# Two graph attention layers on one core: the first layer's product in three f16 parts from packed words in one ring of eight slots

## The chip, the cores and the metric

One Trainium2 chip, one of its cores. The metric is device time in microseconds (us) of one execution, the median of the runs. TensorE is PE in the rows (PEld is its weight load), VectorE is DVE, ScalarE is ACT, GpSimd is POOL, and SyncE is SP, whose queue issues the loads of the adjacency matrix.

## What is computed

x is 8192 x 128 in f32, adj is 8192 x 8192 of 0 and 1 in int32. Cut to what matters:

```python
def layer0(h, adj, W, a):
    wh = h @ W
    e = wh @ a[:128] + (wh @ a[128:]).T
    e = jnp.where(e > 0, e, 0.2 * e)
    att = softmax(jnp.where(adj > 0, e, -9e15), axis=-1)
    return elu(att @ wh)

def layer1(f, adj, Wq, Wk):
    Qn, Kn = unit_rows(f @ Wq.T), unit_rows(f @ Wk.T)
    att = softmax(jnp.where(adj > 0, Kn @ Qn.T, -9e15), axis=1)
    prop = where(row_has_edge, att @ f, f)
    return 0.5 * prop + 0.5 * f

x = x + layer0(relu(layernorm(x)), adj, W, a)
x = x + layer1(relu(layernorm(x)), adj, Wq, Wk)
```

With e = a_i + b_j, the exponential of the leaky sum is the greater of exp(a_i + b_j) and exp(0.2 a_i + 0.2 b_j). Up to a factor of row i, which the quotient of the softmax removes, that is exp(b_j) times the greater of r_i = exp(0.8 a_i) and a threshold of column j, exp(-0.8 b_j). So layer 0 needs no exponential for each pair (i, j).

## The kernel before

**Stages.** LayerNorm of x, a transpose and the projection with W (to about 46 us of the profile), layer 0 (52 to 992 us), the second LayerNorm's transposes and the q and k projections (to about 1075 us), and layer 1 (to the end, 2463.6 us). The change touches layer 0 and the head of it.

**Layer 0.** The 8192 rows i are cut in 8 chunks of 1024 (`C0`), each with 8 accumulators of 128 x 129 in PSUM (`acc0`; two sets, so that the next chunk can start while one is read). For each chunk the kernel goes over the 8192 neighbours j in 64 tiles of 128, two tiles to a step; so a chunk has 32 steps, and layer 0 has 256. A step loads 1 MB of adj into `adj_ring` (4 slots), makes 2 x 1024 weights per partition in `p_ring` (4 slots, f32), and multiplies them with two tiles of `v_buf` (wh with a column of ones, f32).

**Who does what in a step.** DVE makes the weights of the even tile (L762, two per-partition scalars) and then multiplies both tiles by the mask adj > 0 (L770, 2048 elements in one instruction, which counts `s_p` up). ACT makes the odd tile in two operations (L452, L456). PE waits for `s_p` and issues 16 f32 products (L982), 8 row blocks for each tile; each shows in the records as two matmuls and two weight loads. It then counts `s_used` up. After a chunk PE adds a term for rows without an edge (L998, 8 f32 products) and counts `s_acc` up.

**The epilogue of a chunk** (quotient, elu, residual, LayerNorm, split into two f16 halves for layer 1) is cut into pieces that DVE and ACT do between the steps of the next chunk: on DVE `denominators` (L692), `negative` (L697), `residual` (L701, L704), `moments` (L710), `scales` (L609) and `split` (L723, L725), on ACT `quotient` (L403), `exponential` (L409), `root` (L415, with a table load) and `normalised` (L425). In chunk 0 their places on DVE hold eight column sums of `v_buf` (L742).

**SP's queue.** A slot of `adj_ring` is free as soon as DVE has masked it, so a load (L250) waits for `s_p`. At the start of a chunk SP first issues the chunk's first four loads, and then the row factors of the next chunk (L266, 512 KB, a row broadcast to 128 partitions), for which it waits until DVE is through with the chunk before. ACT turns them into r_i (L389). For chunk 0 the row factors don't pass through memory: PE transposes them to PSUM (L949).

**Layer 1** already multiplies in f16 halves: scores (L1050, 512 columns), and then, for each row block, high x high, high x low, low x high (L1067, 129 or 128 columns, weights next to each other in memory). In both layers the loop over chunks is unrolled by two, with a shorter loop inside.

## Time and profile before

| | |
|---|---|
| median of 3 runs | 2465.29 us (2465.23 to 2467.15) |
| span of the profiled execution | 2463.6 us |
| PE busy | 2390.4 us, 97% |
| weight loads busy | 2006.0 us, 81% |
| DVE busy | 2133.0 us, 87% |
| ACT busy | 1756.8 us, 71% |
| DMA in layer 0 | about 300 GB/s, 85% of 16 engines busy |

The span is from the first to the last instruction; the runs' time lies 1.7 us above it. Busy shares are averages over stages; the rows ahead of the prediction are read by stage.

### The profile page before, as it was taken

How to read it: one execution, taken by the hardware profiler on the slowest of the kernel's cores; microseconds unless marked ns; L12 is line 12 of the kernel's file. 1: busy time of each engine (PE TensorE's matmuls, PEld its weight loads, DVE VectorE, ACT ScalarE, POOL GpSimd, SP SyncE). 2: the span in 40 equal slices, each digit the busy share in tenths (PEclk: the TensorE clock that was granted, in tenths of full speed). 3: DMA queues.
4: the chain of work that ended last, by engine and by line, in shares of the span. 5: the costliest groups of instructions: out<-in, count | busy, mean ns of one | idle time of the engine just before them, and what ended most of it. 6: DMA issues, size and time to landing. Idle time of an engine off the chain costs nothing.

```text
span 2463.6 us, 62421 instructions
## 1 busy us (share of the span) xinstructions
PE 2390.4 (97%) x24203; PEld 2006.0 (81%) x24203; DVE 2133.0 (87%) x1653; ACT 1756.8 (71%) x1654; POOL 1.4 (0%) x9
## 2 busy tenths in 40 slices
PE   6999999999999999799999999999999999999999
PEld 5899999999999999667776776776767767767777
DVE  7989898989898988898887888888888878878887
ACT  6567676777777776677776776776777767767776
POOL 0000000000000000000000000000000000000000
PEclk9999999999999999999999999999999999999999
DMA  4798888888888879245565665655655556556563
GB/s 184 256 323 295 304 293 309 304 303 307 299 309 287 318 281 327 68 151 204 203 216 180 210 213 178 217 205 190 213 201 201 202 188 217 192 197 215 205 205 120
DMA packets 153299, 572.05 MB, mean 232 GB/s; under 512 B 9872, under 2 KB 10320, under 8 KB 152784
## 3 DMA queue, kind: packets, MB, share of 16 engines
q1 hardware_dynamic: 143952, 549.26, 63.7%
q10 hardware_dynamic: 9216, 20.98, 2.2%
q8 instruction: 91, 1.49, 0.2%
q14 instruction: 40, 0.33, 0.0%
HBM read 557.58 MB, written 12.62 MB: 231 GB/s over the span
## 4 chain that ended last, share of the span: by engine, by line
PE 91%; DVE 4%; issue 3%; ACT 1%; DMA 0%; SPq 0%; DVEq 0%; ACTq 0%
PE bank L982 35%; PE bank L1067 28%; PE bank L1050 27%; DVE v_sum L742 1%; PE bank L998 1%; DVE hl_buf L620 1%; DVE p_ring L762 0%; DVE hl_buf L802 0%; DVE p_ring L632 0%; PE bank L1009 0%; DVE norm L791 0%; DVE v_buf L809 0%; DVE q_buf L809 0%; PE bank L928 0%; DMA wqk_sb<-wqk 0%
## 5 line engine op out<-in xcount | busy, mean ns | idle before, releaser
L982 PE MATMUL bank<-v_buf,p_ring 128*128 (+1 forms) x8192 | 920.2, 275 | 10.5 <-DVE p_ring L770 6.0
L982 PEld LDWEIGHTS bank<-v_buf,p_ring 128*128 128x128 f32 x8192 | 917.8, 192 | 12.2 <-issue 10.9
L529 ACT ACTIVATE p_ring<-bank 128x1024 f32<-128x1024 f32 x512 | 523.8, 1024 | 386.2 <-PE bank L1050 386.0
L1067 PEld LDWEIGHTS bank<-u_buf,hl_buf 128*128 128x128 f16 x12288 | 721.7, 97 | 61.9 <-issue 2.2
L835 DVE SCALAR_TENSOR_TENSOR p_ring<-adj_ring,p_ring 128x2048 f32<-128x2048 int32 x256 | 586.6, 2292 | 204.4 <-ACT p_ring L529 204.4
L1067 PE MATMUL bank<-u_buf,hl_buf 128*128 (+2 forms) x12288 | 742.7, 220 | 1.2 <-issue 1.1
L1050 PE MATMUL bank<-v_buf,q_buf 128*128 (+1 forms) x3072 | 711.1, 381 | 21.2 <-issue 19.1
L770 DVE SCALAR_TENSOR_TENSOR p_ring<-adj_ring,p_ring 128x2048 f32<-128x2048 int32 x255 | 584.6, 2292 | 75.6 <-DVE p_ring L762 29.9
L840 DVE TENSOR_TENSOR hl_buf<-p_ring,hl_buf 128x2048 f16<-128x2048 f32 x256 | 584.6, 2284 | 0.0
L1050 PEld LDWEIGHTS bank<-v_buf,q_buf 128*128 (+1 forms) x3072 | 291.8, 98 | 329.1 <-issue 29.6
L535 ACT ACTIVATE hl_buf<-p_ring 128x2048 f16<-128x2048 f32 x256 | 487.1, 1903 | 0.6 <-DVE p_ring L835 0.6
L452 ACT ACTIVATE p_ring<-r_ring,ns_col,f_col 128x1024 f32<-128x1024 f32 x256 | 317.6, 1241 | 222.3 <-PE bank L982 211.6
L456 ACT ACTIVATE p_ring<-p_ring,s_col 128x1024 f32<-128x1024 f32 x256 | 294.3, 1150 | 29.6 <-ACT p_ring L452 12.2
L762 DVE TENSOR_SCALAR p_ring<-r_ring,f_col,s_col 128x1024 f32<-128x1024 f32 x256 | 206.7, 808 | 9.5 <-PE bank L982 4.1
L1009 PE MATMUL bank<-wqk_sb,hl_buf 128*128 128x256 f32 x128 | 33.7, 410 | 10.0 <-DVE hl_buf L802 8.9
L1009 PEld LDWEIGHTS bank<-wqk_sb,hl_buf 128*128 128x128 f32 x128 | 24.3, 200 | 16.5 <-ACT hl_buf L471 7.2
L914 PE MATMUL bank<-ident,hl_buf 128*128 128x128 f32 x128 | 20.9, 292 | 9.9 <-DVE hl_buf L620 9.8
L914 PEld LDWEIGHTS bank<-ident,hl_buf 128*128 128x128 f32 x128 | 15.7, 148 | 13.7 <-DVE hl_buf L620 8.3
L403 ACT ACTIVATE hl_buf<-bank,den 128x128 f32<-128x128 f32 x64 | 17.2, 377 | 12.1 <-DVE den L692 12.1
L425 ACT ACTIVATE hl_buf<-q_buf,nbias,rstd 128x128 f32 (+1 forms) x64 | 25.8, 483 | 0.0
L1020 PE MATMUL bank<-ident,hl_buf 128*128 128x128 f32 x128 | 17.7, 283 | 5.7 <-DVE v_buf L809 5.7
L544 ACT ACTIVATE r_ring<-bank,den 128x128 f32<-128x128 f32 x64 | 18.1, 371 | 6.7 <-DVE den L857 6.7
(94 smaller groups left out, 432.6 us busy)
## 6 DMA issues: line engine op xcount, KB each, us to landing
adj_ring<-adj SPq DMA_DIRECT2D x512, 1024.0 KB, 4.9
x_dram<-q_buf ACTq DMA_DIRECT2D x8, 512.0 KB, 5.5
h_dram<-hl_buf ACTq DMA_DIRECT2D x8, 512.0 KB, 5.7
hl_buf<-h_dram SPq DMA_DIRECT2D x16, 256.0 KB, 2.7
r_ring<-x_dram ACTq DMA_DIRECT2D x16, 256.0 KB, 3.7
r_ring<-h_dram ACTq DMA_DIRECT2D x16, 256.0 KB, 3.9
out<-r_ring ACTq DMA_DIRECT2D x16, 256.0 KB, 3.8
r_ring<-a_rows SPq DMA_DIRECT2D x7, 512.0 KB, 5.5
```

The lines of the kernel that those rows point to most:

```text
L452: nc.scalar.activation(dst, row, ACT.Relu, bias=ns_col[:, bass.ds(j, 1)], scale=f_col[:, bass.ds(j, 1)]).then_inc(s_half, 1)
L456: nc.scalar.activation(dst, dst, ACT.Identity, bias=s_col[:, bass.ds(j, 1)]).then_inc(s_odd, 1)
L529: nc.scalar.activation(p_ring[:, k, hf * 1024:(hf + 1) * 1024], bank[:, 2 * hf:2 * hf + 2, :].rearrange("p b n -> p (b n)"), ACT.Exp, scal ...
L535: nc.scalar.activation(hl_buf[:, 0, k, :], p_ring[:, k, :], ACT.Copy).then_inc(s_ph, 1)
L762: V.tensor_scalar(p0(k)[:, :, 0, :], row, f_col[:, bass.ds(j, 1)], s_col[:, bass.ds(j, 1)], ALU.mult, ALU.max).then_inc(s_even, 1)
L770: V.scalar_tensor_tensor(p_ring[:, k, :], adj_ring[:, k, :], 0.0, p_ring[:, k, :], ALU.is_gt, ALU.mult).then_inc(s_p, 1)
L835: V.scalar_tensor_tensor(p_ring[:, k, :], adj_ring[:, k, :], 0.0, p_ring[:, k, :], ALU.is_gt, ALU.mult).then_inc(s_m, 1)
L840: V.tensor_tensor(hl_buf[:, 1, k, :], p_ring[:, k, :], hl_buf[:, 0, k, :], ALU.subtract).then_inc(s_pl, 1)
L982: ins = mm(acc0(par, it), p0(k)[:, it // 4, jj, f], v_buf[:, bass.ds(j * VW, D + 1)], start=start, stop=False, skip_group_check=True)
L1009: ins = mm(qk_banks(r)[:, k * 2 * D:(k + 1) * 2 * D], ht_ring[:, r, k * P:(k + 1) * P], wqk_sb[:, :], start=True, stop=True)
L1050: ins = mm(bank[:, 2 * hf + m, :], q_buf[:, qs, bass.ds(j * P, P)], k_buf[:, ks, bass.ds(i * IW, IW)], start=(x == 0), stop=(x == 2))
L1067: ins = mm(o, hl_buf[:, ps, k, f], v.rearrange("p o c -> p (o c)"), start=head and m == 0 and it % 2 == 0 and (ps, us) == (0, 0), stop=tai ...
```

## The change

**Weights.** The r_i and the thresholds become words of 32 bits: the upper 16 bits are an f16 just below the value (value times 1 - 2^-11), the lower 16 bits are the f16 of what is left (`split_words`). Of two such positive words the greater as an f32 is the word of the greater value. In a step ACT turns the slot's 0 and 1 into 0.0 and 1.0 in place (`ACT.Sign`, 2048 elements), and DVE takes, for each of the two tiles, max(row word, threshold word) * mask in place (two SCALAR_TENSOR_TENSOR of 1024 elements with one per-partition scalar). So a slot holds adj, then the mask, then the weights: there is one `ring` of 8 slots in the place of `adj_ring` and `p_ring`, and layer 1 uses its two halves as before.

**Values.** exp(b_j) goes into the values: `value_scaled`, `value_high` and `value_low` (DVE, ACT, DVE; 16 times each, 4 tiles at a time) turn each tile of `v_buf` into two f16 halves. Two of the 16 are done before the first step, the others between the steps of chunk 0.

**Products.** For each tile PE does 8 row blocks high x high, then 8 high x low, then 8 low x high, all f16 with 129 columns. The weights are read from the words, so each f16 weight lies 4 bytes from the next. The column sums (L742) go: ACT sums the columns of h as it copies them (`accum_out`), DVE adds those sums up, and PE multiplies them with W.

**Queues.** A slot is free when PE has used it, so a load waits for `s_used`. The load of the next chunk's row words is written ahead of the chunk's first loads. The row words of chunk 0 go through memory too. PE's groups in the loop are 8 steps long (they were 4), and the chunks' steps on ACT and DVE are written out without an inner loop.

```diff
-                    for k in range(RING):
-
-                        sp.wait_ge(s_p, RING * (G0 * c + g - 1) + k + 1)
-                        load0(c, RING * g + k, k)
+                    for k in range(RING0):
+
+                        sp.wait_ge(s_used, U0 * c + RING0 * (g - 1) + k + 1)
+                        load0(c, RING0 * g + k, k)
+
+                if not last:
+                    if not first:
+
+                        sp.wait_ge(s_p, U0 * c)
+                    load_r(c + 1, 1 - par)
                 if not first:
                     group(0)
-                if not last:
-                    if not first:
-
-                        sp.wait_ge(s_p, RING * G0 * c)
-                    load_r(c + 1, 1 - par)
...
+                for u in range(U0):
+                    k = u % RING0
+                    act.wait_ge(s_adj[k], 16 * (G0 * c + u // RING0 + 1))
+                    act.nop(nofuse=True)
+                    nc.scalar.activation(slot(k), slot(k, I32), ACT.Sign).then_inc(s_sg, 1)
+                    if u in parts:
+                        parts[u]()
...
+                dve.wait_ge(s_rin[par], 8 * c + 16 - 8 * par)
+                dve.nop(nofuse=True)
+                for u in range(U0):
+                    k = u % RING0
+                    n = U0 * c + u
+                    dve.wait_ge(s_sg, n + 1)
+                    dve.nop(nofuse=True)
+                    for jj in range(2):
+                        half = words0(k)[:, :, jj, :]
+                        ins = V.scalar_tensor_tensor(half, r_ring[:, par, :].rearrange("p (b n) -> p b n", b=2),
+                                                     th_word[:, 2 * u + jj:2 * u + jj + 1], half, ALU.max, ALU.mult)
+                    ins.then_inc(s_p, 1)
+                    if u in parts:
+                        parts[u]()
...
+            def value_scaled(q):
+                if q >= 2:
+                    dve.wait_ge(s_vl, q - 1)
+                f4 = f_col[:, ZT * q:ZT * q + ZT].unsqueeze(2).to_broadcast([P, ZT, D + 1])
+                V.tensor_tensor(vz_ring[:, q % 2, :, :], v0[:, ZT * q:ZT * q + ZT, 0:D + 1], f4,
+                                ALU.mult).then_inc(s_vz, 1)
+
+            def value_low(q):
+                dve.wait_ge(s_vh, q + 1)
+                tiles = v2_tiles[:, ZT * q:ZT * q + ZT, :]
+                V.tensor_tensor(tiles[:, :, VW:VW + D + 1], vz_ring[:, q % 2, :, :], tiles[:, :, 0:D + 1],
+                                ALU.subtract).then_inc(s_vl, 1)
...
+                            for ps, us in parts:
+                                for it in range(IT0):
+                                    start = peeled and k == 0 and jj == 0 and it % 3 == 0
+                                    f = slice((it % 4) * P, (it % 4 + 1) * P)
+                                    ins = mm(acc0(par, it), weights0(k, ps)[:, it // 4, jj, f],
+                                             v2[:, bass.ds((2 * j + us) * VW, D + 1)],
+                                             start=start and (ps, us) == (0, 0), stop=False, skip_group_check=True)
```

The order of the work moves on two queues that the prediction speaks of. On SP, at the start of the loop over pairs of chunks, this stands there before (`weights_ready` is `s_p`, which DVE counts; L250 loads adj, L266 the row factors):

```order
L216 ISA
L278 REGISTER_ALU
L250 ISA [waits weights_ready]
L250 DMA adj_ring<-adj 128x2x1024
L278 REGISTER_ALU
L250 ISA [waits weights_ready]
L250 DMA adj_ring<-adj 128x2x1024
...
L286 REGISTER_ALU
L266 ISA [waits weights_ready]
L266 DMA r_ring<-a_rows 128x1024
```

And this now (`weights_used` is `s_used`, which PE counts; L266 loads adj, L282 the row words):

```order
L232 ISA
L282 ISA [waits weights_ready]
L282 DMA r_ring<-a_rows 128x1024
L296 REGISTER_ALU
L266 ISA [waits weights_used]
L266 DMA ring<-adj 128x2x1024
L296 REGISTER_ALU
L266 ISA [waits weights_used]
L266 DMA ring<-adj 128x2x1024
```

The wait for DVE and the load of the row words moved from behind the chunk's first loads to ahead of them.

On DVE, at the start of chunk 0's steps, this stands there before (L762 and L770 as above, L742 a column sum):

```order
L762 TENSOR_SCALAR p_ring<-r_ring,f_col,s_col 128x2x512
L770 SCALAR_TENSOR_TENSOR p_ring<-adj_ring,p_ring 128x2048 [waits adj_in1,odd_tile_ready,even_tile_ready]
L742 TENSOR_REDUCE v_sum<-v_buf 128x16
L762 TENSOR_SCALAR p_ring<-r_ring,f_col,s_col 128x2x512
L770 SCALAR_TENSOR_TENSOR p_ring<-adj_ring,p_ring 128x2048 [waits adj_in2,odd_tile_ready,even_tile_ready]
```

And this now (L781 the max and mask of one tile, L707 `value_scaled`, L713 `value_low`):

```order
L707 TENSOR_TENSOR hl_buf<-v_buf,f_col 128x516 [waits factors_ready,words_step]
L707 TENSOR_TENSOR hl_buf<-v_buf,f_col 128x516
L713 TENSOR_TENSOR v_buf<-hl_buf,v_buf 128x4x129 [waits values_high] x2
L781 SCALAR_TENSOR_TENSOR ring<-r_ring,th_word,ring 128x2x512 [waits r_in0,mask_ready]
L781 SCALAR_TENSOR_TENSOR ring<-r_ring,th_word,ring 128x2x512
L707 TENSOR_TENSOR hl_buf<-v_buf,f_col 128x516 [waits values_low]
L781 SCALAR_TENSOR_TENSOR ring<-r_ring,th_word,ring 128x2x512 [waits mask_ready]
L781 SCALAR_TENSOR_TENSOR ring<-r_ring,th_word,ring 128x2x512
L713 TENSOR_TENSOR v_buf<-hl_buf,v_buf 128x4x129 [waits values_high]
```

A step has two equal instructions now, and one piece of the values stands behind each step of the first 28.

On PE, the loop body over pairs of chunks holds 2320 f16 products (400 f32 products before), and the shorter loop inside it 384 (64 before).

## Rows read from the trace of the kernel before

**Rows 1.** PE in order of time, layer 0: start us, duration us, engine, line, operation

```profile
118.96 57.44 PE L982 MATMUL bank<-v_buf,p_ring 128*128 x512 [0.80 <-DVE p_ring L770]
176.24 1.95 PE L998 MATMUL bank<-v_sum,empty_w 128*128 128x129 f32 x16
178.02 114.52 PE L982 MATMUL bank<-v_buf,p_ring 128*128 128x129 f32 x1024
292.38 1.95 PE L998 MATMUL bank<-v_sum,empty_w 128*128 128x129 f32 x16
294.17 114.52 PE L982 MATMUL bank<-v_buf,p_ring 128*128 128x129 f32 x1024
...
991.92 1.89 PE L1009 MATMUL bank<-wqk_sb,hl_buf 128*128 128x256 f32 x8
```

**Rows 2.** PE in order of time, two stretches of layer 1

```profile
1202.11 2.75 PE L1050 MATMUL bank<-v_buf,q_buf 128*128 x12
1204.70 2.90 PE L1067 MATMUL bank<-u_buf,hl_buf 128*128 x48
1207.44 2.75 PE L1050 MATMUL bank<-v_buf,q_buf 128*128 x12
...
1317.38 4.39 PE L1050 MATMUL bank<-v_buf,q_buf 128*128 x12 [3.24 <-issue]
1321.56 3.00 PE L1067 MATMUL bank<-u_buf,hl_buf 128*128 128x129 f16 x48
```

**Rows 3.** DVE in order of time, the epilogue's pieces in chunk 3 of layer 0

```profile
429.99 0.69 DVE L697 TENSOR_SCALAR hl_buf<-hl_buf 128x1024 f32<-128x1024 f32 x1
430.59 0.81 DVE L762 TENSOR_SCALAR p_ring<-r_ring,f_col,s_col 128x1024 f32<-128x1024 f32 x1
...
440.38 1.22 DVE L701 SCALAR_TENSOR_TENSOR hl_buf<-hl_buf 128x1024 f32<-128x1024 f32 x1
441.75 1.23 DVE L704 SCALAR_TENSOR_TENSOR q_buf<-hl_buf,q_buf 128x1024 f32 x1 [0.16 <-DVE hl_buf L701]
442.89 0.81 DVE L762 TENSOR_SCALAR p_ring<-r_ring,f_col,s_col 128x1024 f32<-128x1024 f32 x1
```

**Rows 4.** Groups by line: engine, operation, shapes, count | busy us, mean ns | idle before, releaser

```profile
L770 DVE SCALAR_TENSOR_TENSOR p_ring<-adj_ring,p_ring 128x2048 f32<-128x2048 int32 x255 | 584.6, 2292 | 75.6 <-DVE p_ring L762 29.9 <-ACT p_ring L456 18.4 <-issue 18.0
L535 ACT ACTIVATE hl_buf<-p_ring 128x2048 f16<-128x2048 f32 x256 | 487.1, 1903 | 0.6 <-DVE p_ring L835 0.6
L1050 PE MATMUL bank<-v_buf,q_buf 128*128 (+1 forms) x3072 | 711.1, 381 | 21.2 <-issue 19.1 <-ACT p_ring L529 1.2 <-DVE hl_buf L802 0.9
L867 DVE SCALAR_TENSOR_TENSOR r_ring<-r_ring,den 128x128 f32<-128x128 f32 x64 | 18.1, 346 | 0.0
L874 DVE TENSOR_TENSOR r_ring<-r_ring 128x512 f32<-128x512 f32 x16 | 11.0, 685 | 0.0
```

**Rows 5.** All engines in order of time, the head of layer 0

```profile
45.74 0.27 DVE L665 TENSOR_REDUCE ab_max<-v_buf 128x1 f32<-128x64 f32 x1 [5.43 <-ACT v_buf L354]
47.61 0.27 ACT L378 ACTIVATE hl_buf<-bank 64x128 f32<-64x128 f32 x1 [1.90 <-PE bank L952]
47.90 0.55 SPq L260 DMA_DIRECT2D a_rows<-hl_buf  x1
49.77 0.35 SPq L266 DMA_DIRECT2D r_ring<-a_rows  x1
52.04 9.01 PE L982 MATMUL bank<-v_buf,p_ring 128*128 128x129 f32 x64 [4.47 <-DVE p_ring L737]
```

**Rows 6.** DMA issues from 46 to 56 us: KB each, median us from issue to landing

```profile
r_ring<-a_rows SPq DMA_DIRECT2D x1, 512.0 KB, 3.6
```

**Rows 7.** DMA issues from 1090 to 2440 us

```profile
adj_ring<-adj SPq DMA_DIRECT2D x247, 1024.0 KB, 4.8
```

**Rows 8.** Busy time in stretches: length, engines (x instructions), PEclk, DMA share, GB/s

```profile
178.02:294.17 116.15, 116.15 (x1042) 116.15 (x1041) 104.37 (x89) 85.89 (x86) 0.00 (x0) 1.00 0.83 300
412.00:416.00 4.00, 4.00 (x38) 4.00 (x37) 3.84 (x6) 1.75 (x2) 0.00 (x0) 1.00 0.97 349
956.00:960.00 4.00, 4.00 (x38) 4.00 (x37) 3.96 (x4) 2.82 (x3) 0.00 (x0) 1.00 1.04 411
1318.00:1322.00 4.00, 4.00 (x16) 1.70 (x15) 0.00 (x0) 1.22 (x2) 0.00 (x0) 0.57 0.32 130
```

More of the change, by code:

```diff
@@ L32 @@
 RING = 4
+RING0 = 8
 LAG = 3
@@ L347, in copy_h1t @@
                     act.wait_ge(s_wh, g - 1)
-                nc.scalar.activation(ht_ring[:, g % 2, :], bank[:, g % 2, :], ACT.Relu).then_inc(s_h1c, 1)
+                nc.scalar.activation(ht_ring[:, g % 2, :], bank[:, g % 2, :], ACT.Relu,
+                                     accum_out=h_sums[:, g:g + 1]).then_inc(s_h1c, 1)
             def evac1(g):
@@ L436, in chunk @@
                 first = isinstance(c, int) and c == 0
-                last = isinstance(c, int) and c == NC0 - 1
-                parts = {} if first else {(g + 1, 1): part for g, part in enumerate(epilogue(c - 1, 1 - par))}
-                if not last:
-                    parts[SPREAD - 1, 1] = lambda: row_factor(c + 1, 1 - par)
-                def group(g, peeled=False):
-                    for k in range(RING):
-                        n = RING * (G0 * c + g) + k
-                        j = 2 * (RING * g + k) + 1
-                        if not (first and peeled):
-                            act.wait_ge(s_used, n - RING + 1)
-                            act.nop(nofuse=True)
-                        dst = p0(k)[:, :, 1, :]
-                        row = r_ring[:, par, :].rearrange("p (b n) -> p b n", b=2)
-                        nc.scalar.activation(dst, row, ACT.Relu, bias=ns_col[:, bass.ds(j, 1)],
-                                             scale=f_col[:, bass.ds(j, 1)]).then_inc(s_half, 1)
-                        act.wait_ge(s_half, n + 1)
-                        act.nop(nofuse=True)
-                        nc.scalar.activation(dst, dst, ACT.Identity, bias=s_col[:, bass.ds(j, 1)]).then_inc(s_odd, 1)
-                        if isinstance(g, int) and (g, k) in parts:
-                            parts[g, k]()
                 if first:
-                    act.wait_ge(s_r, 1)
-                else:
-                    act.wait_ge(s_r, c + 1)
-                for g in range(SPREAD):
-                    group(g, peeled=(g == 0))
-                with act.Fori(0, G0 - SPREAD) as h:
-                    group(h + SPREAD)
+                    parts = {2 * q - 3: (lambda q=q: value_high(q)) for q in range(2, T // ZT)}
+                    value_high(0)
+                    value_high(1)
+                else:
+                    parts = dict(zip((5, 9, 13, 17), epilogue(c - 1, 1 - par)))
+                for u in range(U0):
[5 more added lines that the diff above has]
+                        parts[u]()
             def copy_ht(g, r):
@@ L678, in _ @@
-            V.tensor_scalar(shift[:, 1:2], shift[:, 0:1], 1.0 - ALPHA, 0.0, ALU.mult, ALU.max).then_inc(s_ab, 1)
-            dve.wait_ge(s_ab, 10)
-            V.tensor_tensor(shift[:, 3:4], shift[:, 3:4], shift[:, 1:2], ALU.subtract).then_inc(s_ab, 1)
-            V.tensor_tensor(shift[:, 4:5], shift[:, 4:5], shift[:, 1:2], ALU.subtract).then_inc(s_ab, 1)
+            top_a, top_nb, top_b = (ab_top[:, i:i + 1] for i in range(3))
+            V.tensor_scalar(ab_col[:, 0, :], ab_col[:, 0, :], top_nb, None, ALU.min).then_inc(s_ab, 1)
@@ new lines, in chunk @@
+                if first:
+                    parts = {2 * q - 4: (lambda q=q: value_scaled(q)) for q in range(2, T // ZT)}
+                    parts |= {2 * q - 3: (lambda q=q: value_low(q)) for q in range(2, T // ZT)}
+                    value_scaled(0)
+                    value_scaled(1)
+                    value_low(0)
+                    value_low(1)
+                else:
+                    parts = dict(zip((3, 7, 10, 11, 15, 19), epilogue(c - 1, 1 - par)))
+                dve.wait_ge(s_rin[par], 8 * c + 16 - 8 * par)
```

219 lines of the change are left out of this document (98 added, 121 removed).

## The prediction

> **What bounds the kernel now.** I read the order of time on PE first. In layer 0 PE works without a gap: a chunk is 114.4 us of L982 and 1.8 us of L998, together 116.15 us, from one chunk's first product to the next's (178.02 to 294.17) [rows 1]. That is 1024 records at 111.7 ns, so 223.4 ns for an f32 product and 3.57 us for a step of 16. In the same stretch DVE is busy 104.4 us, ACT 85.9 us, and the DMA engines move 300 GB/s at a share of 0.83 [rows 8]. So layer 0 goes at PE's pace, with DVE 10% behind it. The stages after it start at 991.92 us [rows 1]; the change leaves them alone, so all that counts is by how much that mark moves.
>
> **PE: the products.** The nearest row for three f16 parts is L1067 in layer 1: 48 products from 1204.70, and the next scores start at 1207.44 [rows 2]. That is 2.74 us, 57.1 ns for a product with its weight load. A step of the changed layer 0 is also 48 f16 products, so 2.74 us, and a chunk is 32 x 2.74 + 1.78 = 89.5 us instead of 116.15. What no row shows is a weight load whose f16 elements lie 4 bytes apart. From below it costs nothing more. From above I take the pace of f32 weight loads, which also read 4 bytes for an element: 111.7 ns. I take 57.1, since both the type and the number of weights are those of L1067.
>
> The Trainium skill, "TensorE: Matmul & The Clock Gate", section "Back-to-back issue gap", puts a sustained stream of pairs of weight load and matmul at about 81 ns each for 128 columns. By it a step would be 3.89 us, above the 3.57 us of f32, and the change would lose 80 us. L1067's row, the same stream but for the spacing of the weights, says 57.1 ns, so the row decides.
>
> **DVE: two instructions a step.** Before, a step is L762 and L770. Now it is two SCALAR_TENSOR_TENSOR of 1024 elements. L704 is one of that size: it starts at 441.75 and the next instruction at 442.89, a pitch of 1.14 us [rows 3]. The new one has a per-partition scalar as well. L867 has one too, at 128 elements: 18.1 us busy for 64, a pitch of 283 ns [rows 4]. Scaled by (1024 - 128) elements at 0.96 a ns that is 1.22 us. So a step is 2.28 to 2.44 us; I take 2.43, as L867 is the same form. The epilogue of a chunk adds its pieces as they show now: 0.6 us for L697, 2.5 us for L701 with L704 [rows 3], and in the same way 0.2, 2.6, 0.3 and 2.0 us for the others, 8.2 us. DVE needs 32 x 2.43 + 8.2 = 86.0 us for a chunk, 3.5 us under PE. ACT's one operation has 2048 elements, as L535: 1.90 us [rows 4], so 61 us and the epilogue's 10. If integer input made it as slow as two of L452 (2 x 1.24 us) it would still be under PE. Pieces that ACT and DVE hand to each other I put at 1.5 us a chunk in waits for DVE (0 to 3).
>
> **SP: what the moved load costs.** This is the step on which the forecast turns. Call D the moment at which DVE ends the last step of a chunk. In the new order SP stands at the wait for D before it may issue the row words, and the next chunk's first loads stand behind them. Their slots came free long before: DVE runs ahead of PE by a few us at most, so at D PE has ended all but two or three of the chunk's steps, and the slots of four or five are free. None of their loads is on its way. From D the chain is: the row words land 3.6 us after their issue when the queue is empty [rows 6]; the load behind them adds 1 MB at the full rate, 2.54 us at 411 GB/s [rows 8]; so it lands at D + 6.3. (From its own 4.8 us [rows 7], the issue of the row words and their 1.3 us of data it comes to 6.8, near enough.) ACT's mask takes 1.95 us with its signal and DVE 2.5 us: the first step of the new chunk is ready at D + 10.9, where it would have been D + 2.4. The next three come at the pace of the loads, 2.54 us. Then DVE goes on at its own pace. From D to the next D:
>
> 10.9 + 3 x 2.54 + 28 x 2.43 + 8.2 + 1.5 = 96.2 us.
>
> That is above PE's 89.5 us, so DVE's chain with the late loads sets the pace of chunks 1 to 6. Chunk 7 has no row words to wait for and goes at PE's pace. PE hides a part of D's delay only where it lags behind DVE; here it catches up in the epilogue, where DVE needs 47.1 us for 16 steps and pieces and PE 43.8 us, and gets 11 x 0.31 = 3.4 us behind again by the chunk's end.
>
> **Head and chunk 0.** Before, PE starts at 52.04 [rows 5]. Now: the row factors on ACT (L378 at 47.61) come some 0.8 us later, behind more small DVE operations; two more of these split them, 0.5 us; the write takes 1.87 us from issue to the next issue (47.90 to 49.77) [rows 5], the row words 3.6 us [rows 6]. DVE starts its first step at 54.4, and PE at 57.0: 5 us later than before. In chunk 0 DVE also has 28 pieces of the values, 516 elements each, 0.62 us by L874 (685 ns [rows 4], less the 0.07 us that neighbours overlap): D at 54.4 + 32 x 2.43 + 17.4 = 149.6. These 17.4 us lie on the path, since nothing covers them.
>
> **Instruction fetch.** The loop over pairs of chunks in layer 1 has PE wait for "issue" 3.24 us once each 175 us, when it goes back, and the next scores take 4.39 us instead of 2.75 [rows 2] at a granted clock of 0.57 [rows 8], a mean of its two levels (1.2 and 2.4 GHz) after the idle time: 4.8 us in all. Layer 0's loop body grows beyond that of layer 1, so it will pay the same, twice, at a chunk's end. There PE waits for the late loads anyway, some 3 us, and it has slack in the epilogue, so I put it at nothing; without that cover it is 9.6 us. The inner loop (384 products) would be fetched anew only if the memory for it were smaller than I think: layer 1's inner loop of 240 also goes back, twice in each of 16 chunks, and all of L1050's waits for issue are 19.1 us [rows 4], six gaps like the one shown.
>
> The Trainium skill, "Runtime: NRT & Kernel Launch", section "Instruction fetch mechanics", gives PE 2048 instructions, which fits both observations, but also speaks of two pages of 16 KiB, by which the inner loop would be fetched anew, 8 times.
>
> **The sum.** D of chunk 0 at 149.6; six periods of 96.2 us give 726.8. PE is 3.4 us behind there, ends its step and L998 (4.5 us), and does chunk 7 in 87.7 + 1.8 + 1.0 us (with the two transposes): 825.2 us. Before it is 991.9. So 166.7 us less: a span of 2296.9 us, and with the 1.7 us that the median lies above the span, **2299 us**. With DVE's step at 2.34 and the delay 1 us shorter it is 2275, with 2.50 and 3 us of waits 2320; that is the likeliest case's own range.
>
> **Rivals.**
> *PE's pace holds.* If DVE's steps take 2.28 us, or the loads come sooner, every chunk is 89.5 us. Chunk 0 ends on PE at 154.2; 154.2 + 7 x 89.5 + 9.6 + 1.0 = 791 us, and the kernel takes 2265 us. For it: PE's row is firm, and DVE is under PE but for the delay. Against it: 8.5 us of delay in each of six chunks against 3.5 us of slack.
> *DVE or the DMA queue is dearer.* At 2.55 us a step it is 28 x 0.12 x 6 + 4 = 24 us more, 2323. The DMA queue must move 32 MB of adj, 1 MB of results and 0.5 MB of row words in a chunk. At 411 GB/s that is 85.5 us; at the 349 GB/s of another full stretch (share 0.97) [rows 8] it is 100.7 us, 4.5 us above the period, 27 us in all, 2326. Both together give 2350. For it: of the two stretches with the queue full that I show, one is that slow. Against it: the other, as long, moves 411.
> *The inner loop is fetched anew.* 8 x 4.8 = 38 us on PE, of which the slack of six chunks takes most: up to 2320, within the cases above.
> *Slower than before: the spaced weights.* If a weight load with 4 bytes between elements is paced like an f32 one, a step is 48 x 111.7 = 5.36 us and the change loses 256 x (5.36 - 3.57) = 458 us: 2923. It decides from 74.5 ns a product on. For it: no row has such a load. Against it: nothing in the rows but the likeness to L1067.
> *The change doesn't do what it says.* If the products went in as f32 pairs or the mask held the slots up, time would stay near 2465; I see nothing for it.
>
> **How the numbers follow.** The forecast (2275 to 2320) has 0.50, PE's pace (2250 to 2275) 0.19, the dearer case (2320 to 2350) 0.24, the spaced weights 0.05, and no effect or a mishap 0.02. The range from 2256 to 2342 leaves out the spaced weights, no effect, and the outermost parts of the two neighbours. A measurement of this kernel can tell 0.2% from no change. Faster by more than that: 0.94; within it 0.01; slower 0.05.
>
> **What would show it.** Right: PE's L982 successor at 57 ns a product; in chunks 1 to 6 a wait of DVE for ACT's mask of some 8 us after the 32nd step, with ACT waiting for DMA, and SP's longest waits on DVE; a period of about 96 us, but 90 in chunk 7. Wrong: a period of 90 us everywhere (PE's pace), a DMA share of 1.0 through the whole chunk (the queue), products well above 57 ns apart (spacing), or waits of "issue" in the middle of a chunk (fetch).

## The result and the profile after

The changed kernel takes 2316.4 us (three executions, 2316.0 to 2318.0) against 2466.2 us (2465.2 to 2467.3): a ratio of 0.9393, interval 0.9378 to 0.9408, 6.1% faster. A fourth execution, of 7992.7 us, is left out as disturbed; with it the median is 2317.2. The forecast was 2299 us with a range of 2256 to 2342. So sign and range held, and the kernel is 17 us slower than forecast. The profiled execution has a span of 2314.2 us; 2296.9 was worked out.

The page of the changed kernel: busy time of the engines, the chain that ended last, and the groups that answer to [rows 4]:

```profile
PE 2195.6 (95%) x28293; PEld 1803.8 (78%) x28293; DVE 1981.7 (86%) x1685; ACT 1632.2 (71%) x1423; POOL 1.4 (0%) x9
...
PE 70%; DVE 13%; issue 8%; DMA 5%; ACT 3%; SPq 0%; DVEq 0%; ACTq 0%; POOL 0%; POOLq 0%
...
L985 PE MATMUL bank<-v_buf,ring 128*128 128x129 f16 (+1 forms) x12288 | 719.6, 222 | 57.7 <-DVE ring L781 55.9
...
L1052 PE MATMUL bank<-v_buf,q_buf 128*128 (+1 forms) x3072 | 713.2, 382 | 21.5 <-issue 19.2
L781 DVE SCALAR_TENSOR_TENSOR ring<-r_ring,th_word,ring 128x1024 f32<-128x1024 f32 x512 | 622.0, 1279 | 89.4 <-ACT ring L464 85.3
...
L464 ACT ACTIVATE ring<-ring 128x2048 f32<-128x2048 int32 x256 | 481.1, 1911 | 131.4 <-DMA ring<-adj 127.2
```

The products of layer 0 are L985 now. They are busy 719.6 us, where the f32 products before filled eight chunks of 114.5 us [rows 1]. But PE stands idle 55.9 us ahead of them for DVE (L781), DVE stands idle 85.3 us for ACT's mask (L464), and ACT 127.2 us for the loads of adj. The row of L1052, in layer 1, is what it was in [rows 4] but for 2 us.

PE in order of time, layer 0, for [rows 1]; in brackets the idle time just before and what ended it. A row names a stretch of one line, xcount is how many matmuls are in it:

```profile
57.42 95.00 PE L985 MATMUL bank<-v_buf,ring 128*128 128x129 f16 x1536 [9.60 <-DVE ring L781]
152.26 2.00 PE L1002 MATMUL bank<-v_sum,empty_w 128*128 128x129 f32 x16
161.99 34.60 PE L985 MATMUL bank<-v_buf,ring 128*128 128x129 f16 x576 [7.73 <-DVE ring L781]
197.59 21.96 PE L985 MATMUL bank<-v_buf,ring 128*128 x384 [1.00 <-DVE ring L781]
...
351.98 2.00 PE L1002 MATMUL bank<-v_sum,empty_w 128*128 128x129 f32 x16
359.71 34.72 PE L985 MATMUL bank<-v_buf,ring 128*128 128x129 f16 x576 [5.73 <-DVE ring L781]
...
748.57 2.00 PE L1002 MATMUL bank<-v_sum,empty_w 128*128 128x129 f32 x16
750.41 65.54 PE L985 MATMUL bank<-v_buf,ring 128*128 128x129 f16 x1152
...
840.31 1.89 PE L1013 MATMUL bank<-wqk_sb,hl_buf 128*128 128x256 f32 x8
```

From the end of chunk 0 (154.10, 1.84 us after L1002 begins, as between 748.57 and 750.41) to the first product of chunk 7 (750.41) it is 596.3 us, 99.4 for each of the chunks 1 to 6. Each of them begins with a gap of 4.4 to 7.7 us, ended by DVE. Chunk 7 (750.41 to 840.31) has no gap and takes 89.9 us, where a chunk took 116.15 before. The next stage starts at 840.31, not at 991.92 [rows 1]; 825.2 was worked out.

SP's waits (us in total, times, longest):

```profile
SPq L266 <- PE bank L985: 478.7, 199, 11.2
SPq L282 <- DVE ring L781: 90.1, 6, 18.5
```

L282 is the load of the row words. Six times, 15.0 us each on average, SP stands there until DVE has ended the last step of a chunk, with the next chunk's first loads behind it. All engines in order of time show what that costs, at the start of chunk 2:

```profile
243.86 2.48 DVE L781 SCALAR_TENSOR_TENSOR ring<-r_ring,th_word,ring 128x1024 f32<-128x1024 f32 x2
...
246.51 0.34 SPq L282 DMA_DIRECT2D r_ring<-a_rows  x1
247.12 9.80 SPq L266 DMA_DIRECT2D ring<-adj  x8
...
254.76 1.91 ACT L464 ACTIVATE ring<-ring 128x2048 f32<-128x2048 int32 x1 [14.31 <-DMA ring<-adj]
256.77 6.41 DVE L781 SCALAR_TENSOR_TENSOR ring<-r_ring,th_word,ring 128x1024 f32<-128x1024 f32 x5 [10.44 <-ACT ring L464]
...
259.31 3.00 PE L985 MATMUL bank<-v_buf,ring 128*128 128x129 f16 x26 [4.42 <-DVE ring L781]
```

DVE ends chunk 1 at 246.34 (the forecast's D). SP issues the row words 0.2 us later and then loads of adj, seven of them within 5 us; the profile shows a wait for PE only ahead of the eighth. So most slots had been free before their loads were issued. The first has landed at 254.76, when ACT starts, having waited 14.3 us. This is D + 8.4; the forecast had D + 6.3. DVE starts at 256.77 and has the first step, two instructions at a pitch of 1.196 us, at 259.2: D + 12.8 instead of D + 10.9.

In chunks 1, 3 and 5 one more thing lies in this chain. The same view, chunk 3, where D is 345.43:

```profile
353.87 1.28 ACT L464 ACT_TABLE_LOAD   x1 [14.09 <-DMA ring<-adj]
```

Behind an ACT_TABLE_LOAD of 1.28 us the first step is ready at D + 14.1. Over the six chunks it is 13.5, 12.8, 14.1, 13.0, 14.3 and 13.1 us, on average 13.5.

Windows for [rows 8] (length, then busy time of PE, PEld, DVE, ACT, POOL with instructions, PE's granted clock, DMA share, GB/s):

```profile
154.10:252.89 98.79, 89.43 (x1539) 88.93 (x1537) 84.66 (x88) 69.13 (x52) 0.00 (x0) 0.97 0.91 359
360.00:364.00 4.00, 4.00 (x43) 4.00 (x41) 4.00 (x4) 2.81 (x2) 0.00 (x0) 0.54 1.02 406
649.23:748.57 99.34, 91.90 (x1555) 91.23 (x1553) 91.64 (x94) 77.94 (x57) 0.00 (x0) 0.97 1.02 405
748.57:838.47 89.90, 89.90 (x1564) 89.88 (x1561) 78.53 (x83) 62.94 (x52) 0.00 (x0) 1.00 0.96 372
```

DMA issues from 180 to 740 us, for [rows 6, 7] (KB each, median us to landing):

```profile
ring<-adj SPq DMA_DIRECT2D x183, 1024.0 KB, 9.3
...
r_ring<-a_rows SPq DMA_DIRECT2D x5, 512.0 KB, 4.4
```

In chunk 1 no engine is busy for the whole 98.8 us: PE is busy 89.4, DVE 84.7, ACT 69.1. After its gap PE also runs slowly, at a granted clock of 0.54 in 360 to 364, a mean near the lower of its two levels (1.2 and 2.4 GHz). A load of adj lands 9.3 us after its issue, where one in layer 1 took 4.8 [rows 7]. The DMA queue is full outside SP's standstill: its share is 0.91 over chunk 1 and 1.02 over chunk 6 (649.23 to 748.57), at whose end there is no standstill. Both chunks are nearly equally long, so the queue doesn't set the period.

### The profile page after: what moved, and what is told of

The parts are those of the page before. It is cut to its first block, busy times and chain, and to the rows that moved or that the text cites. A ratio compares the mean times of both kernels' runs of the same rounds, so it can differ in the third digit from the quotient of the medians.

```text
span 2314.2 us, 69259 instructions
## 1 busy us (share of the span) xinstructions
PE 2195.6 (95%) x28293; PEld 1803.8 (78%) x28293; DVE 1981.7 (86%) x1685; ACT 1632.2 (71%) x1423; POOL 1.4 (0%) x9
## 3 DMA queue, kind: packets, MB, share of 16 engines
q8 instruction: 155, 2.54, 0.4%
## 4 chain that ended last, share of the span: by engine, by line
PE 70%; DVE 13%; issue 8%; DMA 5%; ACT 3%; SPq 0%; DVEq 0%; ACTq 0%; POOL 0%; POOLq 0%
PE bank L1069 30%; PE bank L1052 29%; PE bank L985 10%; DVE ring L781 9%; DMA ring<-adj 4%; ACT ring L464 1%; ACT hl_buf L440 1%; DVE hl_buf L806 1%; DVE stats L742 0%; DVE norm L795 0%; SPq L266 0%; ACT hl_buf L418 0%; DVE hl_buf L733 0%; PE bank L1013 0%; DVE v_buf L813 0%
## 5 line engine op out<-in xcount | busy, mean ns | idle before, releaser
L528 ACT ACTIVATE ring<-bank 128x1024 f32<-128x1024 f32 x512 | 523.8, 1024 | 387.5 <-PE bank L1052 387.3
L985 PE MATMUL bank<-v_buf,ring 128*128 128x129 f16 (+1 forms) x12288 | 719.6, 222 | 57.7 <-DVE ring L781 55.9
L985 PEld LDWEIGHTS bank<-v_buf,ring 128*128 128x128 f16 x12288 | 713.0, 99 | 64.5 <-DVE ring L781 34.2
L839 DVE SCALAR_TENSOR_TENSOR ring<-ring 128x2048 f32<-128x2048 int32 x256 | 586.6, 2291 | 205.8 <-ACT ring L528 205.8
L1052 PE MATMUL bank<-v_buf,q_buf 128*128 (+1 forms) x3072 | 713.2, 382 | 21.5 <-issue 19.2
L781 DVE SCALAR_TENSOR_TENSOR ring<-r_ring,th_word,ring 128x1024 f32<-128x1024 f32 x512 | 622.0, 1279 | 89.4 <-ACT ring L464 85.3
L844 DVE TENSOR_TENSOR hl_buf<-ring,hl_buf 128x2048 f16<-128x2048 f32 x256 | 584.5, 2283 | 0.0
L464 ACT ACTIVATE ring<-ring 128x2048 f32<-128x2048 int32 x256 | 481.1, 1911 | 131.4 <-DMA ring<-adj 127.2
L1052 PEld LDWEIGHTS bank<-v_buf,q_buf 128*128 (+1 forms) x3072 | 292.0, 98 | 330.9 <-issue 32.2
L534 ACT ACTIVATE hl_buf<-ring 128x2048 f16<-128x2048 f32 x256 | 487.1, 1903 | 0.6 <-DVE ring L839 0.6
L440 ACT ACTIVATE hl_buf<-q_buf,nbias,rstd 128x128 f32 (+1 forms) x64 | 25.9, 485 | 14.3 <-DVE nbias L610 14.3
L408 ACT ACTIVATE v_buf<-hl_buf 128x516 f16<-128x516 f32 x16 | 10.2, 641 | 27.1 <-DVE hl_buf L707 27.1
L918 PEld LDWEIGHTS bank<-ident,hl_buf 128*128 128x128 f32 x128 | 15.7, 149 | 13.5 <-DVE hl_buf L619 8.1
```

The lines of the kernel that those rows point to most:

```text
L440: ins = nc.scalar.activation(h_buf[:, it * P:(it + 1) * P], xs[:, bass.ds(c * C0 + it * P, P)], ACT.Relu, bias=nbias[:, it:it + 1], scale= ...
L464: nc.scalar.activation(slot(k), slot(k, I32), ACT.Sign).then_inc(s_sg, 1)
L528: nc.scalar.activation(p_ring[:, k, hf * 1024:(hf + 1) * 1024], bank[:, 2 * hf:2 * hf + 2, :].rearrange("p b n -> p (b n)"), ACT.Exp, scal ...
L534: nc.scalar.activation(hl_buf[:, 0, k, :], p_ring[:, k, :], ACT.Copy).then_inc(s_ph, 1)
L781: ins = V.scalar_tensor_tensor(half, r_ring[:, par, :].rearrange("p (b n) -> p b n", b=2), th_word[:, 2 * u + jj:2 * u + jj + 1], half, AL ...
L839: V.scalar_tensor_tensor(p_ring[:, k, :], adj_ring[:, k, :], 0.0, p_ring[:, k, :], ALU.is_gt, ALU.mult).then_inc(s_m, 1)
```

## The experiments

The theory is the forecast's: in chunks 1 to 6 SP's wait for D, with the loads queued behind it, sets the pace. The rivals are the transfer of the row words itself, DVE's work, the DMA queue, and PE's products. The names of the lines of layer 0 are as in the changed kernel (L781 DVE's weights, L464 ACT's mask, L985 the products); where an edit adds lines ahead of them the numbers are a few higher.

**e1_rows_behind.** SP's order as it was before, first the loads, then the wait and the row words.

```diff
+                if not first:
+                    group(0)
                 if not last:
...
                     load_r(c + 1, 1 - par)
-                if not first:
-                    group(0)
```

> The changed kernel with one edit: the load of the next chunk's row words, and the wait for DVE ahead of it, stand behind the chunk's first eight loads again. My theory: the gaps of 4.4 to 7.7 us that PE has at the start of chunks 1 to 6 come from this wait. Without it chunks 1 to 6 go at PE's pace, 87.2 + 1.8 = 89.0 us instead of 99.4, plus 4.8 us twice for instruction fetch: about 53 us less, 2264 us. Rival 1, DVE's work and its epilogue are the bound: the gaps move into the chunk and the time stays above 2300. Rival 2, the DMA queue is the bound: its share is 1.0 through whole chunks and the time is 2285 or more.

Measured: 2263.2 us, ratio 0.9173 (0.9158 to 0.9188), 53 us less than the changed kernel, as the theory had it (2264). PE in order of time:

```profile
243.31 87.34 PE L985 MATMUL bank<-v_buf,ring 128*128 128x129 f16 x1536
330.48 2.00 PE L1002 MATMUL bank<-v_sum,empty_w 128*128 128x129 f32 x16
335.89 88.97 PE L985 MATMUL bank<-v_buf,ring 128*128 128x129 f16 x1536 [3.41 <-issue]
...
519.88 88.97 PE L985 MATMUL bank<-v_buf,ring 128*128 128x129 f16 x1536 [4.17 <-issue]
```

And a window in chunk 2 of it:

```profile
243.31:330.48 87.17, 87.17 (x1539) 87.17 (x1536) 77.09 (x83) 69.38 (x53) 0.00 (x0) 1.00 1.02 399
```

PE's gaps at the chunks' starts, which DVE ended, are gone, and chunks 1, 2, 4 and 6 take 89.0 us. So the wait's place cost 53 of the 203 us that this version gains. DVE's work (77 us of 87) doesn't hold PE up. Neither does the DMA queue, but it is close: it moves 399 GB/s here at a share of 1.02, so half of the second rival's sign is there, and only the time (2263 and not 2285) speaks against it. At the 411 GB/s of [rows 8] a chunk's bytes need 85.5 us, an estimate, 3.5 us less than PE. At chunks 3 and 5 a part of the gap stays. There PE goes back in its loop over pairs. It waits 3.4 and 4.2 us for "issue", which the forecast had put under the cover of the late loads, and the 1536 products take 1.63 us longer. With a few tenths between instructions that is 5.2 and 6.0 us.

**e2_rows_small.** The changed kernel, with SP's wait where it is, but from chunk 2 on only 128 of the 1024 columns of row words are loaded. The remaining columns are left as they were, so the weights of those chunks are not the reference's.

```diff
+            def load_r_part(c, par):
+                row = a_flat[bass.ds(c * C0, P)].rearrange("(o n) -> o n", o=1)
+                sp.dma_start(r_ring[:, par, 0:P], row.to_broadcast([P, P])).then_inc(s_rin[par], 16)
...
-                    load_r(c + 1, 1 - par)
+                    (load_r if first else load_r_part)(c + 1, 1 - par)
```

> The changed kernel, with the wait and the order of its queue kept, but from the row words of chunk 2 on only 128 of the 1024 columns are loaded (the others keep old values, so this part of the computation is left out). It parts the wait from the transfer behind it. My theory: the wait for DVE is the cost, and the transfer adds only its 1.1 us of data for each of five or six chunks: 2309 to 2312 us. Rival: it is the transfer itself, whose 4.5 us to landing lie ahead of the first load: 25 us less, 2292 us.

Measured: 2308.7 us, ratio 0.9356 (0.9340 to 0.9371), 8 us less than the changed kernel. That is the theory's size (2309 to 2312) and not the rival's (2292), and far from the 53 us of e1. All engines in order of time, start of chunk 3:

```profile
345.37 8.78 SPq L266 DMA_DIRECT2D ring<-adj  x8
...
351.45 1.28 ACT L468 ACT_TABLE_LOAD   x1 [13.49 <-DMA ring<-adj]
```

From the issue of the first load to ACT's start it is 6.1 us here, and 6.5 on average over the six chunks (5.7 to 7.3); in the changed kernel it was 7.6 (247.12 to 254.76), and 7.6 on average as well. So the row words' bytes cost about 1.1 us a chunk, as expected, and what e1 gained beyond that is the wait. (At chunk 5 this run has a gap of 4.81 us for "issue" in place of one for DVE, as e1 has.) It also shows that a load which is the first of some six in a row needs some 6.5 us with hardly anything ahead of it, where a load of layer 1 needs 4.8 [rows 7]. That those behind it take part of the DMA engines' time is what I suppose; no run here issues it alone at that place.

**e3_row_blocks.** On e1, the products of a tile row block by row block, each with its three products.

```diff
-                            for ps, us in parts:
-                                for it in range(IT0):
+                            for it in range(IT0):
+                                for ps, us in parts:
```

> The kernel e1_rows_behind with the products of a tile in the other order: for each row block high x high, high x low, low x high, as layer 1 has them. There PE is the bound, so its pace shows. My theory: a product takes 56.8 ns in either order, and the time is that of e1_rows_behind within 0.2%. Rival: three products in a row into one accumulator, two of them with the same weights, are slower (2 ns each would be 25 us) or, with the weights kept, faster.

Measured: 2270.0 us, ratio 0.9196 (0.9181 to 0.9212), 6.9 us above e1 (0.3%). The expectation of no difference is missed. The two intervals overlap a little, but the traces part them. PE, chunk 1 of it:

```profile
154.42 88.30 PE L985 MATMUL bank<-v_buf,ring 128*128 128x129 f16 x1536
242.56 2.00 PE L1002 MATMUL bank<-v_sum,empty_w 128*128 128x129 f32 x16
```

From the first product to L1002 it is 88.14 us, 57.4 ns a product. Product by product, in e1, it is 87.17 us, 56.8 ns. In a chunk that goes at PE's pace that is 0.96 us, 6.7 in the seven behind chunk 0, where DVE sets the pace. Both orders read the same weights and values; why the one is 0.6 ns dearer no view says.

**e4_table_early.** The changed kernel, with a Sign of one column on ACT at the head of each chunk from 1 on, so that the table is loaded while ACT has nothing to do.

```diff
                 first = isinstance(c, int) and c == 0
+                if not first:
+                    nc.scalar.activation(warm[:, :], ident[:, 0:1], ACT.Sign)
```

> The changed kernel with one tiny Sign on ACT at the head of each chunk but the first, so that the table load that stands ahead of the mask in chunks 1, 3 and 5 is done while ACT waits for the first load. My theory: the late loads' chain sets the pace, and 1.3 us of table load lies on it in each of these three chunks: 3.8 us less, 2313 us. Rival: PE or the DMA queue sets it, and nothing changes.

Measured: 2310.1 us, ratio 0.9362 (0.9347 to 0.9378), 6 us less than the changed kernel, where 3.8 was expected. The two intervals just touch. In its profiled execution, which was 2316.1 us and so the longest of the four, PE in order of time has:

```profile
162.88 31.44 PE L987 MATMUL bank<-v_buf,ring 128*128 128x129 f16 x528 [6.41 <-DVE ring L783]
...
360.96 34.11 PE L987 MATMUL bank<-v_buf,ring 128*128 128x129 f16 x576 [4.23 <-issue]
```

The gap ahead of chunk 1 is 6.41 us instead of 7.73, which is the table load's 1.28. Ahead of chunk 3 the table's gain is not seen: there PE now waits for "issue", the fetch that DVE's lateness covered in the changed kernel. From PE's first product to the end of layer 0 this execution takes 782.6 us, the changed kernel's 782.9. So the profile shows no gain. In it the first steps come 4.8 us sooner in six chunks, 12.7 us behind D on average instead of 13.5. But DVE then waits 2.2 us more for masks within the chunks, and the period between two loads of row words falls only from 98.9 to 98.7 us (150.79 to 644.24 in five). What made the other three executions 6 us faster no trace shows, so what the table load costs isn't settled.

**e5_weights_adjacent.** On e1, the weights are read 2 bytes apart instead of 4. They are then the words' halves mixed, not the f16 values: the computation is another, the work is the same.

```diff
-            return slot(k, F16).rearrange("p (b j n s) -> p b j n s", b=2, j=2, s=2)[:, :, :, :, 1 - part]
+            half = slot(k, F16)[:, (1 - part) * STEP:(2 - part) * STEP]
+            return half.rearrange("p (b j n) -> p b j n", b=2, j=2)
```

> The kernel e1_rows_behind with each f16 weight read next to the one before it (2 bytes apart) in place of 4 bytes apart. It reads the halves of the slot as they lie, so the products mix high and low words: this part of the computation is changed. There PE is the bound. My theory: the spacing costs nothing, a product stays at 56.8 ns and the time within 0.2% of e1_rows_behind (2263). Rival: the spaced weights cost something, and adjacent ones are faster by 1 ns a product or more, 2250 or less.

Measured: 2265.4 us, ratio 0.9180 (0.9165 to 0.9196), e1 within its interval. Its chunk 1 has 87.33 us of products, e1's 87.34. The spacing of the weights costs nothing, and the rival of the forecast that put it at 458 us falls with a measurement of its own.

**e6_pe_unrolled, e10_pe_unrolled_again.** On e1, PE's loop over pairs of chunks is written out, so PE never goes back; e10 is the same kernel once more, beside e9.

```diff
-            chunks0(pe, chunk)
+            for c in range(NC0):
+                chunk(c, c % 2)
```

> The kernel e1_rows_behind with PE's loop over pairs of chunks in layer 0 written out, so that PE never jumps back over a chunk pair; the short inner loops stay. My theory: the two gaps of 3.4 and 4.2 us at the start of chunks 3 and 5, with the slow stretch behind each, are code fetched anew after the jump back, and both go: 5.2 + 6.0 = 11 us less, 2252 us. Rival: they come from late weights (DVE or DMA) and stay, or the longer straight code brings gaps of its own: 2263 or more.

> The kernel e6_pe_unrolled once more, so that the next one has its partner on the same chip. Theory: 2257 us within 0.1%, chunk 0 again 94.8 us long on TensorE, with DVE's waits at the starts of the later chunks between nothing and 2 us each. Rival (its time hangs on a slack of a few tenths of a microsecond that differs from run to run): over 3 us off, in the chunk starts.

Measured: 2257.0 us, ratio 0.9151 (0.9135 to 0.9166), and 2257.8, ratio 0.9155 (0.9139 to 0.9170). The waits for "issue" are gone, but only 6 us of the 11 came. PE in order of time in e10, chunks 3 and 5:

```profile
366.42 21.96 PE L985 MATMUL bank<-v_buf,ring 128*128 x384 [1.05 <-DVE ring L781]
...
547.91 21.96 PE L985 MATMUL bank<-v_buf,ring 128*128 x384 [1.89 <-DVE ring L781]
```

PE begins these chunks 3.4 and 6.7 us earlier than in e1, and meets DVE in the middle of the epilogue's pieces, after 12 steps. Five such waits of 0.4 to 1.9 us, 4.6 in all, stand where e1 has none. Where DVE's lag comes from shows on DVE and ACT in the same execution, at the start of chunk 3:

```profile
318.73 1.28 ACT L464 ACT_TABLE_LOAD   x1 [0.62 <-DMA ring<-adj]
320.02 3.72 ACT L464 ACTIVATE ring<-ring 128x2048 f32<-128x2048 int32 x2
...
329.12 9.66 DVE L781 SCALAR_TENSOR_TENSOR ring<-r_ring,th_word,ring 128x1024 f32<-128x1024 f32 x8 [6.21 <-ACT ring L464]
```

The table load stands ahead of the chunk's first mask, which is done at 321.9. DVE ends chunk 2 at 322.9 and begins chunk 3 only at 329.12. So it stands still for 6.2 us with its input ready; that the row puts this down to ACT is wrong. At the start of chunk 5 it is 5.9 us. In e1, e3, e5, e6 and e8 the same two standstills are 6.0 to 6.8 us long; at the starts of chunks 2, 4, 6 and 7 of e10 there is none. DVE, like PE, goes back in its loop over pairs at chunks 3 and 5. A fetch of code on DVE would fit; no run changes DVE's loop, so the cause stays open. In e1 PE's own fetch covered this standstill, as in the changed kernel the late loads covered both.

**e7_pool_values and e9_act_values.** Both on e6: the 14 `value_scaled` that stand between DVE's steps of chunk 0 go to GpSimd (e7, the same tensor_tensor) or to ACT (e9).

```diff
-                    parts = {2 * q - 4: (lambda q=q: value_scaled(q)) for q in range(2, T // ZT)}
-                    parts |= {2 * q - 3: (lambda q=q: value_low(q)) for q in range(2, T // ZT)}
+                    parts = {2 * q - 3: (lambda q=q: value_low(q)) for q in range(2, T // ZT)}
```

in e9, with on ACT:

```diff
+                if q >= 2:
+                    act.wait_ge(s_vl, q - 1)
+                    act.nop(nofuse=True)
+                    for t in range(ZT):
+                        ins = nc.scalar.activation(vz_ring[:, q % 2, t, :], v0[:, ZT * q + t, 0:D + 1], ACT.Copy,
+                                                   scale=f_col[:, ZT * q + t:ZT * q + t + 1])
+                    ins.then_inc(s_vz, 1)
```

> The kernel e6_pe_unrolled with the scaling of 14 of the 16 groups of values moved from DVE to GpSimd, which is idle. My theory: in chunk 0 DVE's 28 pieces lie on the path; without 14 of them DVE needs 8.7 us less there and PE's pace (87.2 us) takes over, so chunk 0 goes from 94.9 us to about 88 and the time falls by 6 to 7 us from e6_pe_unrolled, to 2245. Rival: GpSimd and DVE get in each other's way at SBUF, or GpSimd is too slow for one piece in 6 us, and chunk 0 stays at 95 us or grows.

> e6_pe_unrolled with the same 14 scalings of chunk 0 on ACT instead of DVE (in the run before they went to GpSimd). The theory, that chunk 0 is bound by DVE's work and that GpSimd's beside it made DVE's steps dearer: here nothing runs on GpSimd, DVE has 14 x 0.61 = 8.6 us less, ACT has 64 ACTIVATEs less in chunk 0 than it could do (it is busy some 72 of 94.9 us) and takes 14 pieces of about 1 us: chunk 0 falls from 94.9 to about 88 us, and the whole to about 2250 us. Rival (ACT's masks become late): chunk 0 stays at 94 us or grows, with DVE waiting for ACT in it, and the whole is at 2257 us or above.

Measured for e7: 2253.9 us, ratio 0.9139 (0.9123 to 0.9154); 2245 was expected. Chunk 0 takes 96.0 us on PE, not less than e6's 94.9. DVE's group in 60 to 150 us, in e10 and then in e7 with GpSimd's beside it:

```profile
L781 DVE SCALAR_TENSOR_TENSOR ring<-r_ring,th_word,ring 128x1024 f32<-128x1024 f32 x63 | 77.6, 1277 | 0.0
```

```profile
L787 DVE SCALAR_TENSOR_TENSOR ring<-r_ring,th_word,ring 128x1024 f32<-128x1024 f32 x61 | 83.6, 1431 | 0.0
...
L360 POOL TENSOR_TENSOR hl_buf<-v_buf,f_col 128x516 f32<-128x516 f32 x12 | 23.5, 1956 | 50.7 <-DVE v_buf L720 50.7
```

DVE has 14 pieces less but its own instructions are 154 ns longer on average, 9.8 us over 64, more than the 8.6 us that it was relieved of. The instructions of this line one by one, shortest, median and longest in ns:

```profile
L787 DVE SCALAR_TENSOR_TENSOR ring<-r_ring,th_word,ring x61: 1271/1275/2072, 59.3 to 149.0; 128x1024 f32<-128x1024 f32 x61
```

Most are as long as before (in e10 none is over 1280 ns, in e6, the same kernel, none over 1339), and some take 0.8 us more. The mean's surplus, 61 x 156 ns = 9.5 us, is twelve times that, and GpSimd has 12 pieces in this stretch. For the piece from 79.85 to 81.81 us it is the one instruction that begins at 80.8, 2065 ns long. The piece takes 1.96 us on GpSimd, as far as the profile can tell there, and 0.61 on DVE.

Measured for e9: 2244.1 us, ratio 0.9097 (0.9082 to 0.9112), 13.7 us less than e10 on the same chip; 2250 was expected. DVE's group in the same stretch:

```profile
L787 DVE SCALAR_TENSOR_TENSOR ring<-r_ring,th_word,ring 128x1024 f32<-128x1024 f32 x69 | 83.9, 1289 | 0.0
```

And PE in order of time:

```profile
56.99 88.82 PE L991 MATMUL bank<-v_buf,ring 128*128 128x129 f16 x1536 [9.60 <-DVE ring L787]
...
147.50 87.34 PE L991 MATMUL bank<-v_buf,ring 128*128 128x129 f16 x1536
...
771.47 1.89 PE L1020 MATMUL bank<-wqk_sb,hl_buf 128*128 128x256 f32 x8
```

DVE's instructions keep their length, chunk 0 falls from 95.0 to 88.8 us, and all chunks behind it go at 89.0 without a gap: layer 0 ends at 771.47, 12.6 us before e10's 784.06. Of these, 0.8 is an earlier first product, 6.2 chunk 0, and the other 5.6 lie behind chunk 0, where e10 has its 4.6 us of waits within the chunks. They are absent in e9, and so is most of DVE's standstill. At the start of chunk 3 e9 has:

```profile
317.70 9.66 DVE L787 SCALAR_TENSOR_TENSOR ring<-r_ring,th_word,ring 128x1024 f32<-128x1024 f32 x8 [0.91 <-ACT ring L471]
```

That is 0.9 us instead of 6.2, and 2.8 instead of 5.9 at chunk 5; in e7 it is 1.5 and 0.7. DVE's loop is the same in all of them. In e7 and e9 its code ahead of the loop is 14 pieces shorter; whether that is the reason was not measured apart. So nearly half of e9's gain in layer 0, and all of e7's, is not what was predicted for them. e9 is faster than both kernels, 9.0% under the one before.

**e8_ring_of_four.** On e1, layer 0 uses 4 slots of the ring instead of 8. PE's and SP's groups become 4 steps long with it.

```diff
-RING0 = 8
+RING0 = 4
```

> The kernel e1_rows_behind with layer 0 in a ring of four slots in place of eight. A slot then goes round in: load 4.8 to 6 us, mask 1.95, max 2.5, products 2.7 us and signals. My theory: that is 12.5 to 13.5 us for four steps, 3.1 to 3.4 us a step against PE's 2.73, so 256 steps take 100 to 170 us longer: 2360 to 2430 us. Rival: four slots do, since the loads overlap, and the time stays within 1% of 2263.

Measured: 2461.4 us, ratio 0.9979 (0.9967 to 0.9991); 2360 to 2430 was expected. PE's group from 200 to 700 us, and the window of the same stretch:

```profile
L985 PE MATMUL bank<-v_buf,ring 128*128 (+1 forms) x6502 | 405.9, 226 | 87.0 <-DVE ring L781 86.5
```

```profile
200.00:700.00 500.00, 412.80 (x6566) 399.15 (x6563) 365.96 (x384) 296.90 (x226) 0.00 (x0) 0.95 0.82 298
```

PE waits 86.5 us in 500 for DVE, at 298 GB/s. A slot goes round in PE's use, load, mask, weights: in one round of this trace it was 13.1 us for four steps, 3.3 a step, which is above PE's 2.74. Where DVE and ACT also do pieces of the epilogue, PE's steps begin 4.1 to 5.0 us apart (307.64, 311.72, 315.89, 320.80, 325.81), since these pieces now lie in the round too. The expectation had left them out. Nearly the whole gain of the change hangs on the eight slots, and these are there since the mask and the weights take the place of adj in its own slot.

## Why the prediction was right, and where it was off

**The products (right).** 57.1 ns was taken from L1067 [rows 2]; in e1 87.17 us for 1536 in a chunk is 56.8 ns. The Trainium skill, "TensorE: Matmul & The Clock Gate", section "Back-to-back issue gap", has about 81 ns for such a pair; no run here shows that, and the trace's row was the better guide. The spaced weights cost nothing (e5).

**DVE's steps (right).** One instruction starts 1.196 us behind the one before, so a step takes 2.39 us for the forecast's 2.43; a piece of the values takes 0.61 for 0.62. PE began at 57.4 (57.0 forecast), D of chunk 0 was at 148.4 (149.6).

**SP's moved wait (the mechanism right, the size off).** This is the term of the sum that was too small. The forecast put the first step of a chunk at D + 10.9 us; it came at 13.5 on average, 2.6 late six times, 15.4 us in all. Layer 0 ended 15.1 us later than worked out. Two parts made it:
- The load landed at D + 8.4, not 6.3. I added 1 MB at the full rate to the row words' landing (3.6 + 2.54), and took the check from the 4.8 us of a load of layer 1 [rows 7] as near enough. Those loads are issued one at a time. Here six or more follow each other within a few microseconds, and the first of them takes 6.5 us on average with next to no row words ahead of it (e2) and 7.6 with them.
- In chunks 1, 3 and 5 ACT loads its table in that chain, 1.28 us. It was not in the sum at all. The trace of before had table loads of 1.28 us in the epilogue; that a new function in the step brings one into a place where ACT waits for a load had to be asked. It delays the first step, by 0.6 us in the average above; but e4's trace shows hardly any of it in the period.

The period between two row word loads was 98.9 us (148.58 to 642.85 in five) for 96.2. The steps, 28 at 0.04 less, took 1.1 off; DVE's waits for ACT within the chunks added about as much (14.1 us in six chunks, 2.4 each, where 1.5 was put). These two errors happen to cancel.

**PE hides a part of it (right).** PE was to start each of the chunks 1 to 6 late, and does. Chunk 7 was to go at PE's own pace, in 90.5 us, and takes 89.9.

**Instruction fetch (right for PE).** The forecast had 4.8 us twice and put them at nothing for their cover. In the changed kernel no wait for "issue" shows on PE in layer 0. In e1 the cover is gone and the two fetches cost 5.2 and 6.0 us, and with PE's loop written out (e6) they are gone. The profile doesn't always name them: in e3 PE's wait of 4.20 us at chunk 3 is put down to DVE, whose first step was ready 5.8 us before PE began. The inner loop of 384 products is not fetched anew: chunk 1 of e1 goes through it without a gap. DVE's standstill of about 6 us at the same two places was not in the forecast at all. It cost nothing in the changed kernel, as DVE waits 11.8 and 12.0 us for the late loads there, so that the sum came out without it is luck. The Trainium skill, "Runtime: NRT & Kernel Launch", section "Instruction fetch mechanics", speaks of 2048 instructions for PE: the loop body over pairs with its 2320 products, each with a weight load, pays at each return, and the inner loop of 384 doesn't, so the trace agrees. The same section's two pages of 16 KiB, by which the inner loop would be fetched anew, no trace here bears out.

**The rivals.** PE's pace was given 2265 us; with the wait undone e1 takes 2263.2. So that rival had the right price, and what kept it from coming true is the wait. DVE was not dearer (2.39 us a step). The DMA queue: the share of 1.0 that was named as its sign is there in chunk 6 of the changed kernel and in e1, but at 405 and 399 GB/s, not the 349 of the slower stretch [rows 8], and it holds up neither. The other stages take 1473.9 us of the span (2314.2 less 840.31) for 1471.7 before. These are 2 us that the forecast didn't have, and the last of the 17.

## What to carry to other kernels

A wait that is moved ahead on a queue costs what is queued behind it: list the loads there, ask since when their slots have been free, and follow the first of them through every engine up to the one that sets the pace, with its landing time in a burst and not alone. A gap that goes uncovers the next: here late loads covered a fetch on PE and a standstill of DVE, and the fetch covered the standstill, so each repair gave less than its own row said. A table load on the way may be such a covered gap too (e4). Before believing what a row names as the end of a wait, look when that engine's work was done. When an engine gets 1.3 times as fast, count the slots as well: with four instead of eight the faster products gave 0.2%.
